# A graph network on one core: the order of TensorE's first-layer products and of ScalarE's tasks in the dense stage

## The reference

```
h = jnp.maximum(_layernorm(x, axis=-1), 0.0); x = x + L0(h)   # graph convolution 128 -> 256 -> 128, self-loops
h = jnp.maximum(_layernorm(x, axis=-1), 0.0); x = x + L1(h)   # two mean-aggregating layers
h = jnp.maximum(_layernorm(x, axis=-1), 0.0); x = x + L2(h)   # three layers with edge attributes and layer norm
h = jnp.maximum(_layernorm(x, axis=-1), 0.0); x = x + L3(h)   # four attention layers, two heads
```

## Time and profile before

| what | value |
|---|---|
| median of three runs | 5929.92 us (5915.99 to 5935.2) |
| the profiled execution | 5922.51 us, span 5920.8 us |
| busy: PE, DVE, ACT, POOL | 72%, 65%, 45%, 61% of the span |
| granted TensorE clock, mean over the span | 0.883 of full speed |
| plain stage | from about 88 to 1570 us, 98 steps |

### The profile page before, as it was taken

One profiled execution on the slowest core, in us unless ns is written; L12 is line 12 of the kernel. 1 busy time (PEld: TensorE's weight loads), 2 busy tenths in 40 slices (PEclk: granted clock), 3 DMA queues, 4 the chain that ended last, 5 costly groups with the idle time before them and its releaser, 6 DMA issues. The chain is left out here.

```text
span 5920.8 us, 124056 instructions
## 1 busy us (share of the span) xinstructions
PE 4245.6 (72%) x28221; PEld 3542.7 (60%) x28462; DVE 3835.5 (65%) x13671; ACT 2674.3 (45%) x6722; POOL 3618.6 (61%) x4389
## 2 busy tenths in 40 slices
PE   3777777777698669888989887649765865940365
PEld 2555555555487557677888776648665854830364
DVE  5666666666666876686666798239537824966465
ACT  2555555555444433366666687213332321410243
POOL 2445444445476757676757573766675576667687
PEclk9888888988899879999999999989998998975566
DMA  2444444444355867685434465854693485479232
GB/s 74 149 156 148 152 151 148 154 156 155 125 148 147 228 195 205 189 252 162 117 97 119 115 176 143 270 180 113 186 288 88 111 275 177 114 246 395 74 104 82
DMA packets 1087162, 971.96 MB, mean 164 GB/s; under 512 B 113211, under 2 KB 845968, under 8 KB 1087030
## 3 DMA queue, kind: packets, MB, share of 16 engines
q1 hardware_dynamic: 992950, 805.93, 43.8%
q0 software_dynamic: 94080, 164.48, 11.0%
HBM read 489.22 MB, written 484.70 MB: 164 GB/s over the span
## 5 line engine op out<-in xcount | busy, mean ns | idle before, releaser
L1022 POOL DMA_INDIRECT G<-table,idx_all x1568 | 1544.9, 985 | 746.8 <-issue 480.9
L1022 POOL DMA_INDIRECT G<-table,idx_l x588 | 606.9, 1032 | 287.3 <-issue 177.4
L1718 PE MATMUL PS<-G,S 128*128 (+2 forms) x3528 | 662.4, 298 | 25.7 <-DMA G<-table,idx_all 11.7
L972 POOL DMA_INDIRECT XIN<-in_x,idx_x x196 | 189.5, 967 | 687.7 <-ACT GN L2111 541.4
L1718 PEld LDWEIGHTS PS<-G,S 128*128 128x128 f32 x3528 | 559.7, 211 | 40.8 <-issue 22.3
L1718 PE MATMUL PS<-G,FS 128*65 (+2 forms) x2646 | 427.8, 298 | 212.1 <-DVE den L1561 124.4
L2111 ACT ACTIVATE CR<-PS 65x128 f32<-65x128 f32 (+1 forms) x882 | 237.7, 270 | 728.3 <-PE PS L1718 723.6
L1718 PE MATMUL PS<-CR,LO 97*128 97x128 f32 (+1 forms) x3528 | 518.7, 294 | 64.9 <-ACT CR L2111 64.8
L1718 PEld LDWEIGHTS PS<-CR,LO 97*128 97x128 f32 x3528 | 476.7, 209 | 76.7 <-ACT CR L2111 76.5
L1715 PE MATMUL PS<-ident,G 128*128 128x128 f32 x1372 | 248.0, 294 | 359.4 <-ACT G L2111 330.0
L1718 PEld LDWEIGHTS PS<-G,FS 128*65 128x65 f32 x2646 | 321.4, 149 | 290.1 <-issue 258.4
(11 more groups left out here) (343 smaller groups left out, 10431.9 us busy)
## 6 DMA issues: line engine op xcount, KB each, us to landing
table<-G SPq DMA_DIRECT2D x392, 256.0 KB, 2.6
table<-RO SPq DMA_DIRECT2D x343, 260.0 KB
table<-RO SPq DMA_DIRECT2D x245, 256.0 KB
XIN<-xrows SPq DMA_DIRECT2D x196, 256.0 KB
F<-table SPq DMA_DIRECT2D x168, 260.0 KB
table<-OWN SPq DMA_DIRECT2D x147, 260.0 KB
OWN<-table SPq DMA_DIRECT2D x124, 260.0 KB
S<-table SPq DMA_DIRECT2D x100, 260.0 KB
```

What stands on the lines that cost most here:

```text
L972: g.indirect_dma_start(M[:, j, :], None, x, bass.IndirectOffsetOnAxis(ap=idx_x[:, t:t + 1], axis=0)).then_inc(gat[j].sem, 16)
L1022: g.indirect_dma_start(G[:, t, 0:w], None, TAB[s], bass.IndirectOffsetOnAxis(ap=idx[:, t:t + 1], axis=0)).then_inc(gat[t % 4].sem, 16)
L1718: return nc.tensor.matmul(o, l, r, start=start, stop=stop)
```

## The change

On TensorE the two first-layer products (hidden, reading UT) are moved ahead of the second stretch's transposes (turned q2), and the third stretch's transposes (turned q3) ahead of the product with OT (sampled). On ScalarE the order of the copies follows (H1T before OT, U before the copy of the sampled product), the root of the first norm is moved ahead of the sampled product's copy, and the edge rows' norm (x_norm) is moved from before that root to behind the copy of the first residual (convolved). Nothing is added or left out.

```
@@ -1815,11 +1815,11 @@
             def plain(m, b):
                 q0, q1, q2, q3 = (earlier((m, 0, b), k) for k in range(4))
                 turned(q1, 1)
-                turned(q2, 2)
                 hidden(q1, 0)
                 hidden(q1, 1)
+                turned(q2, 2)
+                turned(q3, 3)
                 sampled(q2)
-                turned(q3, 3)
                 convolved(q1)
                 attributes(q2)
                 rows_b(q2)
@@ -2189,14 +2189,14 @@
             def plain(m, b):
                 q0, q1, q2, q3 = (earlier((m, 0, b), k) for k in range(4))
                 turned(q1, 1)
+                hidden(q1)
                 turned(q2, 2)
-                hidden(q1)
+                turned(q3, 3)
+                root(q0, 1)
                 sampled(q2)
-                turned(q3, 3)
-                x_norm(q2)
-                root(q0, 1)
                 norm(q0, 1)
                 convolved(q1)
+                x_norm(q2)
                 x_root(q1)
                 rows_a(q2)
                 root(q1, 2)
```

## The result

The changed kernel takes 5994.8 us (median of 4 runs, 5993.3 to 6002.7), the kernel before 5929.2 on the same chip: a ratio of 1.0116, 95% interval 1.0097 to 1.0136. It is slower by about 66 us, where 36 were forecast. The direction and the wide range (5926 to 6026) held; the size was nearly double, and the time lies just above the 5949 to 5990 that the prediction gave to its own case.

The account below looks back on a forecast made before the run. Bound by the loop from ScalarE's copy into UT over TensorE, ScalarE and VectorE back to ScalarE. 48 pairs x 0.76 us = 36 us, on 5922.5 profiled gives 5959, plus 7.4 gives 5966 us; own range 5949 to 5990, wide range 5926 to 6026.

Parts of the forecast that it names:

- its own case: The forecast itself: 5966 us, slower by 0.76 us for a pair of steps, chance 0.50.
- The early root by itself: Even step: the root ahead of the sampled copy removes VectorE's 3.33 us wait, gaining at most 1.02 us for a pair.
- First-layer products ahead of the transposes: TensorE: no gain from going first; transposes and copy into OT now delay the sampled product, +0.76 us for a pair.
- The middle case: Half clock lasts through the transposes: products with w2 start at 5.98 us; odd step +0.11, even step +0.65.
- the case with the sampled product too at half: Half clock also on the sampled product: products with w2 start at 6.82 us; odd step +0.95, even step +1.49.
- The even step's +0.65: Even step: the second residual starts at 9.24 instead of 8.59 us, behind TensorE's later products with w2.
- VectorE's wait for the root: Sign: VectorE's idle time before the first norm's reciprocal in even steps, 3.33 us, gone or below 1 us.
- The edge norm's cover on ScalarE: Edge norm's 1.65 us ahead of rows_a hidden by VectorE's 2.34 us of work; costed at nothing, about 0.1 us spare.
- I cost it at nothing: Odd step: later gathers leave 3.0 us for edge rows to land; costed at nothing, 1.3 us at the upper bound.
- Rival 3: Edge rows land late, delaying VectorE's statistics and H1T in the odd step: +1.2 us for a pair, 6023 us; chance 0.10.
- TensorE's order in the odd step: Odd step: products with w2 start at 5.98 instead of 5.87 us, +0.11 of the pair's +0.76.
- rival 4: Half clock throughout, the sampled product included: +2.44 us for a pair, 6047 us; chance 0.08.

Follow-up runs that it names:

- both_early: Kernel before, with the edge norm directly behind the copy into OT and the first norm's root ahead of the sampled product's copy; 5877.8 us, ratio 0.9913.
- norm_late_alone: Kernel before with one edit, the edge rows' norm moved behind the copy of the first residual; 5943.2 us, ratio 1.0044.
- before_filled: Kernel before, plus two unused sampled products on TensorE ahead of each step's first transposes; 5903.8 us, ratio 0.9958.
- both_early_filled: both_early plus two unused sampled products on TensorE ahead of each step's first transposes; 5879.6 us, ratio 0.9905 to the kernel before.

## Why the prediction was right, and where it was not

*What bounds the kernel.* Right: the loop from the copy into UT. The early root by itself was bounded at 1.02 us for a pair; both_early, where it comes with an early edge norm, gained 1.07. Half of that is in the odd step (15.95 to 15.43), which the prediction did not have. Its account of that step leaves out that VectorE's statistics of x wait there for the load of x, in the kernel before (first line, the first product at 1007.10) and, for less long, in both_early (the other two):

```profile
1010.05 0.87 DVE L1226 BATCH_NORM_STATS2 G<-G 128x6 f32<-128x128 f32 x4 [1.63 <-DMA G<-in_x]
```

```profile
713.96 3.44 PE L1718 MATMUL PS<-UT,w 128*128 128x512 f32 x4 [0.23 <-ACT UT L2111]
...
715.87 0.87 DVE L1226 BATCH_NORM_STATS2 G<-G 128x6 f32<-128x128 f32 x4 [0.52 <-DMA G<-in_x]
```

The load is issued 1.15 us ahead of the first product in both kernels. In the medians of the odd steps its rows are read 2.0 to 2.1 us behind the first product in the five kernels with the early edge norm, and 2.5 to 2.9 in the seven others. So this half of the gain goes with the edge norm and not with the root. That the load lands sooner because the gathers then lie further ahead of it was not tested.

*First-layer products ahead of the transposes.* Right that they gain nothing by going first, 0.05 us behind the copy. The middle case put the products with w2 at 5.98; the median of the even steps is 5.78, and the step shown has 6.65, close to the 6.82 of the case with the sampled product too at half. The cases were the right ones: the sampled product starts 5.37 us behind the first (1133.75 - 1128.38), behind the copy into OT, and the first residual has got its wait for TensorE, 2.08 us. The even step's +0.65 became +0.59, the one term that was sized well. The third transposes just fit into the wait for the copy, as it says: the copy into OT ends at 1133.66, and TensorE goes on from the eight transposes to the sampled product without a wait. One sign failed: VectorE's wait for the root was to be gone or below 1 us and is 1.77, because on ScalarE the root stands behind the copies into OT and U, which wait for the late transposes. It cost nothing in this step, where the residual waits for TensorE after it.

*The edge norm's cover on ScalarE.* Right: costed at nothing, and norm_late_alone shows the even step shorter with the norm there. In the changed kernel the cover is just used up, as forecast: the aggregation ends at 1140.52, and ScalarE's next root starts at 1140.56.

```profile
1140.15 0.37 DVE L1234 BATCH_NORM_AGGREGATE G<-G 128x2 f32<-128x6 f32 x4
```

```profile
1140.56 0.30 ACT L2111 ACTIVATE G<-G,eps 128x4 f32<-128x4 f32 x1
```

*The step that failed: "I cost it at nothing", of the edge rows' landing.* The times before it were right: the gathers follow the norm by 0.77 us and end 1.36 us behind the odd step's first product, 1.2 in the prediction. But the rows take 3.42 us to land where 3.0 were left, and VectorE would have come for them earlier than before, 3.69 us behind the first product (1147.95 - 1144.26) instead of 4.22. Each alone would have shown; together they make the wait of 1.08. The trace of before only gave 4.28 as an upper bound, and the value taken was the convenient end of that range. By the prediction's own sign ("or if VectorE waits for the edge rows") it is wrong here. Rival 3, with a chance of 0.10, was this mechanism: VectorE waits 1.14 us in the mean pair, which costs 0.46 us of a pair where it is taken away rather than 1.2, since TensorE was late in the same place. The wide range held because it reached past this rival, not because the forecast's own sum was complete.

*TensorE's order in the odd step.* With the edge norm early the odd step is still 0.22 longer than before and the even step 0.78, 1.00 together, against 0.76 in the sum. So of the 70 us between the two profiled executions, 48 x 1.00 = 48 are TensorE's order less the root's gain, where 36 were forecast, and 48 x 0.46 = 22 are the edge rows, where nothing was.

*The clock.* The change took the transposes out of the gap, and rival 4 weighed that a longer gap could bring more half clock. The granted clock did fall, from 0.87 to 0.84 in the stage, short of rival 4's case. That the clock is what makes this order dear was in the cases of the sum; the added products showed it, with the 1.6% that fell to 0.5% and the full-clock steps that are as short in either order. The Trainium skill's advice (TensorE: Matmul & The Clock Gate, section Why this matters for your kernels) to leave no idle gaps between bursts of matmuls is borne out by before_filled, with 0.87 to 0.94.

## What to carry to other kernels

When an instruction is moved later, follow what it releases on the queues behind it (here a gather that reuses its buffer) to the reader of the data, and count the landing at its bound unless a row shows less. Before putting work on the critical path out of an idle gap, look at the clock of what follows the gap: here the order that cost 1.6% of the time cost 0.5% when the gap was filled. The waits that remain on an engine are places for short, early-ready instructions: the norm and the root, put into two of them under TensorE's old order, gained 0.9%, where the change as a whole lost 1.2%.

## What was not expected of the hardware

Useless matmuls made the kernel faster. Two 128x512 products for each step raised TensorE's granted clock from 0.87 to 0.94, cut the mean first-layer product from 1013 to 736 ns and the run by 0.42%, though nothing waits for them. A half-clock stretch that is driven from one group can fall on another: in both_early_filled it came to lie on products with w2 in some odd steps, 3.62 us instead of 2.02, until that wait was filled as well.
